# A gated cross-attention block with its feed-forward: the mask as one row, row maxima in fp16, constants and squares moved, the down product one unit further behind

## What is computed

```
logits  = einsum(Q, K) + b[0] + -1e30 * (1 - mask)
weights = softmax(logits);  out = weights @ V
x = x + tanh(g_xattn) * attention(ctx, layernorm(x), mask)
gate = x' @ wg.T / 127 ; up = x' @ wu.T / 127      # x' = layernorm(x)
x = x + tanh(g_ffn) * (silu(gate) * up) @ wd.T / 127
```

## Time and profile before

| what | value |
|---|---|
| median of 3 runs | 160.29 us (159.06 to 160.47) |
| the profiled execution | 158.84 us, span 157.0 us |
| PE busy | 132.8 us (85%) in 1363 matmuls |
| VectorE (DVE) busy | 122.4 us (78%) in 348 |
| ScalarE (ACT) busy | 92.9 us (59%) in 203 |
| GpSimd (POOL) busy | 90.9 us (58%) in 139 |
| mean granted TensorE clock | 0.994 |

### The profile page before, as it was taken

How to read it: one execution, slowest core, us unless ns; L and a number is a source line. 1 busy time by engine, 2 the same in 40 slices (tenths; PEclk the granted TensorE clock), 3 DMA queues, 4 the chain that set the end, 5 groups by cost and what they waited for, 6 DMA issues and landing times.

```text
span 157.0 us, 4000 instructions
## 1 busy us (share of the span) xinstructions
PE 132.8 (85%) x1363; PEld 99.9 (64%) x1363; DVE 122.4 (78%) x348; ACT 92.9 (59%) x203; POOL 90.9 (58%) x139
## 2 busy tenths in 40 slices
PE   0656789957898997999899999998999998899970
PEld 0233557735477685858695878678777777676750
DVE  3799899999998988997899699567924937766631
ACT  4327789967556483738373748553877654465530
POOL 6254450542755794689465956645674678774530
PEclk9999999999999999999999999999999999999997
DMA  4499910000006002921171216250100020020022
GB/s 134 134 364 373 363 44 0 6 0 0 4 0 134 6 19 48 136 71 34 33 138 67 40 33 134 71 69 0 43 28 0 0 71 0 0 69 4 0 73 75
DMA packets 19928, 11.06 MB, mean 70 GB/s; under 512 B 13488, under 2 KB 19136, under 8 KB 19904
## 3 DMA queue, kind: packets, MB, share of 16 engines
q1 hardware_dynamic: 19728, 10.49, 25.6%
q10 hardware_dynamic: 176, 0.27, 0.5%
HBM read 5.51 MB, written 2.10 MB: 48 GB/s over the span
## 4 chain that ended last, share of the span: by engine, by line
PE 34%; DVE 27%; POOL 12%; DMA 11%; issue 10%; ACT 3%; SPq 1%; POOLq 0%; DVEq 0%; ACTq 0%
PE ps L1339 13%; DMA n_t<-norm 8%; PE ps L1361 6%; DVE neg_max L1019 4%; DVE stats L911 4%; DVE gated L1068 3%; DMA gates<-in_L_xattn_b_dram 3%; POOL norm L675 3%; POOL rstd L646 3%; POOL norm L668 2%; PE ps L1274 2%; PE ps L1268 2%; DVE x_sb L890 2%; PE ps L1288 2%; DVE h L1079 2%
## 5 line engine op out<-in xcount | busy, mean ns | idle before, releaser
L1339 PE MATMUL ps<-n_t,w_gu_t 128*128 128x256 f16 x384 | 49.9, 273 | 3.3 <-DMA n_t<-norm 2.2
L1339 PEld LDWEIGHTS ps<-n_t,w_gu_t 128*128 128x128 f16 x384 | 36.2, 98 | 13.1 <-DMA n_t<-norm 4.2
L692 POOL TENSOR_TENSOR h<-h 128x256 f16<-128x256 f32 x48 | 32.2, 673 | 15.0 <-ACT h L832 14.8
L823 ACT ACTIVATE tanh_h<-ps 128x256 f32<-128x256 f32 x48 | 18.3, 382 | 21.0 <-PE ps L1339 20.8
L1361 PE MATMUL ps<-w_d_t,h 128*128 128x256 f16 x192 | 28.3, 272 | 0.8 <-DVE x_sb L890 0.4
L1019 DVE TENSOR_REDUCE neg_max<-ps 128x4 f32<-128x512 f32 x32 | 21.5, 685 | 6.5 <-PE ps L1218 6.5
L1068 DVE SCALAR_TENSOR_TENSOR gated<-tanh_h,ps 128x256 f32<-128x256 f32 x48 | 19.7, 411 | 6.1 <-ACT tanh_h L823 6.1
L646 POOL TENSOR_TENSOR rstd<-var_eps,neg_half 128x2 f32<-128x2 f32 x16 | 11.1, 696 | 21.4 <-DVE var_eps L918 21.3
L776 ACT ACTIVATE probs<-ps,key_bias 128x512 f32<-128x512 f32 x32 | 21.9, 684 | 2.5 <-PE ps L1247 2.4
L832 ACT ACTIVATE h<-h 128x256 f16<-128x256 f32 x48 | 19.8, 412 | 5.7 <-DVE h L1079 5.2
L1079 DVE SCALAR_TENSOR_TENSOR h<-ps,gated 128x256 f32<-128x256 f32 x48 | 20.3, 424 | 1.7
(11 more groups left out here) (97 smaller groups left out, 203.8 us busy)
## 6 DMA issues: line engine op xcount, KB each, us to landing
x_sb<-in_x_dram SPq DMA_DIRECT2D x8, 256.0 KB, 8.8
out_dram<-x_sb SPq DMA_DIRECT2D x8, 256.0 KB, 2.1
kv<-in_ctx_dram SPq DMA_DIRECT2D x3, 256.0 KB, 8.3
w_raw<-in_L_ffn_w_gate_dram SPq DMA_DIRECT2D x1, 768.0 KB, 7.3
w_raw<-in_L_ffn_w_up_dram SPq DMA_DIRECT2D x1, 768.0 KB, 9.1
w_raw<-in_L_ffn_w_down_dram SPq DMA_DIRECT2D x1, 768.0 KB, 8.4
kv<-in_ctx_dram ACTq DMA_DIRECT2D x1, 256.0 KB, 3.5
q_stacks<-q_parts SPq DMA_TRANSPOSE x8, 3.2
```

Of the source, the lines that this page charges most:

```text
L692: pool.tensor_tensor(h16[:, r % 2, m, 1, :], h32[:, n % NHB, :], h16[:, r % 2, m, 0, :], ALU.subtract).then_inc(h_low, 1)
L823: act.activation(tanh_h[:, n % 2, :], bank32(HID_BANKS[n % 2])[:, 0:SH], ACT.Tanh, scale=0.5 * W_SCALE).then_inc(tanh_done, 1)
L1339: ins = pe.matmul(dst, lhs, rhs, start=(w == 0 and (k, l) == terms[0]), stop=(k, l) == terms[-1], skip_group_check=True)
```

## The change

- **Mask.** The last 128 mask values of each batch are loaded once more as one row on one partition (`mask_row`, issued on ACT's queue ahead of the old mask load) and turned by one DVE step (`bias_row`) into 0 or -42496 in bf16. The mask matmul of `row_max` now has this one row and one row of ones as operands (contraction of 1 instead of 128), still 512 columns. The exp takes `exp_bias` (per key, four columns), made by `mask_t` and `exp_bias`, two small steps later on. The three-part bf16 split (`mask_parts`), the transposes and ACT copy of `mask_rows` leave the narrow path.
- **Maxima.** The reduction writes the negated maximum straight as fp16 (`max_cols16`); `max_split` leaves the narrow path, and `max_t` transposes fp16 and waits for the last reduction. The selector is fp16 too. `K_LIMIT` falls to 7500 (a constant in one clamp and one scale).
- **Order of the opening.** `k_parts 0` moves ahead of `norm1 0` on DVE, its low part from POOL to DVE (`k_rest`); 30 warm-up matmuls in six places (8, 2, 4, 4, 9, 3) stand for the 8 in one place, the first group before any other PE work; the mask transpose moves behind `q_stack 0 1`.
- **Loads.** The load of the keys and values of batch 0 moves from ACT's queue to SP's, behind the first x load; the three gates' loads move behind x 1 and kv 1.
- **Squares.** The ten square sums, one a chore, move from stages 0 to 1 to stages 3 to 6 (every second chore), `check` and `flag_sum` behind them to stage 6. `y_scale` stays where it was.
- **LAG** is 4 instead of 3; for the last six units the distance is 5 as before.
- One more memset (`max_cols16`) at the start of DVE.

```diff
-WARM_UP = 8
-K_LIMIT = 60000.0
+WARM_UP = (8, 2, 4, 4, 9, 3)
+K_LIMIT = 7500.0
+SHUT_OUT = -42496.0
...
-    steps = [("stats", 1, 0), ("mask_t",), ("warm_up",), ("norm1", 0), ("high", 1, 0), ("low", 1, 0), ("k_parts", 0),
-             ("mask_parts",), ("mask_rows",), ("dup", 0), ("stats", 1, 1), ("q_stack", 0, 0), ("k_stack", 0),
-             ("norm1", 1), ("q_stack", 0, 1), ("high", 1, 1), ("low", 1, 1), *maxima(0)[:3], ("dup", 1),
-             *maxima(0)[3:], sq(0), ("q_stack", 0, 2), ("max_split", 0), ("max_t", 0), ("q_stack", 0, 3),
-             ("k_parts", 1), ("stats", 1, 2)]
-
-    chores = [[sq(1)], [("w_cast", 0)], [sq(2), sq(3)], [("k_stack", 1)], [("w_t", 0), sq(4)],
-              [("w_cast", 1), ("w_t", 1), sq(5)],
-              [sq(6), sq(9)], [("w_t", 2)], [sq(7), ("w_t", 3)], [sq(8), ("check",)], [("flag_sum",), ("y_scale",)], [("w_cast", 2)],
-              [("w_t", 4)], [("w_t", 5)], [], [("k_parts", 2)], [("k_stack", 2)]]
+    steps = [("bias_row",), ("stats", 1, 0), ("warm_up", 0), ("k_parts", 0), ("norm1", 0), ("k_rest", 0),
+             ("high", 1, 0), ("low", 1, 0), ("mask_cast",), ("dup", 0), ("warm_up", 1), ("k_stack", 0),
+             ("stats", 1, 1), ("warm_up", 2), ("q_stack", 0, 0), ("q_stack", 0, 1), ("mask_t",), ("norm1", 1),
+             ("high", 1, 1), ("low", 1, 1), ("warm_up", 3), *maxima(0)[:2], ("exp_bias",), maxima(0)[2], ("dup", 1),
+             *maxima(0)[3:], ("warm_up", 4), ("q_stack", 0, 2), ("max_t", 0), ("q_stack", 0, 3), ("k_parts", 1),
+             ("stats", 1, 2), ("warm_up", 5)]
+
+    chores = [[], [("w_cast", 0)], [], [("k_stack", 1)], [("w_t", 0)], [("w_cast", 1), ("w_t", 1)],
+              [], [("w_t", 2)], [("w_t", 3)], [], [("y_scale",)], [("w_cast", 2)],
+              [("w_t", 4)], [("w_t", 5)], [], [("k_parts", 2)], [("k_stack", 2)], []]
+    chores += [part for i in range(10) for part in ([], [sq(i)])] + [[("check",)], [("flag_sum",)]]
...
-    LAG = 3
+    LAG = 4
...
-        put(("max_split", r + 1), when=ahead)
...
-        unit(n + i, LAG if i < 9 else LAG + 2)
+        unit(n + i, LAG if i < 9 else LAG + 1)
...
             load_x(sp, 0)
+            load_kv(sp, 0)
+            load_x(sp, 1)
+            load_kv(sp, 1)
             for n, g in enumerate((g_xattn, g_ffn, attn_b)):
                 sp.dma_start(gates[:, n:n + 1], g.partition_broadcast(P)).then_inc(gates_loaded, 16)
-            load_x(sp, 1)
-            load_kv(sp, 1)
...
+            act.dma_start(mask_row[:, :, :], mask[:, LAST * P:SK].unsqueeze(0)).then_inc(mask_row_loaded, 16)
             act.dma_start(mask_raw[:, :], mask.rearrange("b (c k) -> (b c) k", k=P)).then_inc(mask_loaded, 16)
-            load_kv(act, 0)
...
+            def exp_bias_steps():
+
+                dve.wait_ge(gates_loaded, 48)
+                mine(dve.tensor_scalar(exp_bias[:, :], exp_bias[:, :], MASK_STEP, gates[:, 2:3], ALU.mult, ALU.add))
+                wait_mine()
+
+                dve.tensor_scalar(exp_bias[:, :], exp_bias[:, :], gates[:, 2:3], 0.0, ALU.subtract, ALU.min
+                                  ).then_inc(exp_bias_ready, 1)
...
+                    elif kind == "bias_row":
+
+                        dve.wait_ge(mask_row_loaded, 16)
+                        dve.tensor_scalar(bias_row[:, :, :], mask_row[:, :, :], -SHUT_OUT, SHUT_OUT, ALU.mult, ALU.add
+                                          ).then_inc(bias_row_ready, 1)
...
+                    elif kind == "k_rest":
+
+                        b = step[1]
+                        dve.wait_ge(k_high, b + 1)
+                        full, high, low = key_parts(b)
+                        dve.tensor_tensor(low, full, high, ALU.subtract).then_inc(k_low, 1)
...
-                        rows = bias_rows[:, b * NC + c, :].unsqueeze(1).to_broadcast((P, HG, P))
-                        pe.matmul(bank32(n), ones_b[:, :], rows, start=False, stop=True, skip_group_check=True
+                        if is_wide:
+                            ones, rows = ones_b[:, :], bias_rows[:, b * NC + c, :].unsqueeze(1).to_broadcast((P, HG, P))
+                        else:
+                            pe.wait_ge(bias_row_ready, 1)
+                            ones, rows = ones_b[0:1, :], bias_row[:, b, :].unsqueeze(1).to_broadcast((1, HG, P))
+                        pe.matmul(bank32(n), ones, rows, start=False, stop=True, skip_group_check=True
```

More of the change, by code:

```diff
@@ L263, in narrow_steps @@
             put(("n_t", h))
-        unit(n + i, LAG if i < 9 else LAG + 2)
+        unit(n + i, LAG if i < 9 else LAG + 1)
         product(n + i)
     for n in range(len(units) + 1, len(units) + LAG + 2):
-        unit(n, LAG + 2)
+        unit(n, LAG + 1)
     return steps, split
@@ L274, in wide_steps @@
     R = 2 * B
-    steps = []
+    steps = [("mask_parts",)]
     for b in range(B):
@@ L379, in flamingo_block_kernel @@
         recip = sb("recip", [P, 2, NH], F32)
+        mask_row = sb("mask_row", [1, B, P], I32)
+        bias_row = sb("bias_row", [1, B, P], BF16)
+        exp_bias = sb("exp_bias", [P, B], F32)
+        max_cols16 = sb("max_cols16", [P, QT, P], F16)
+        max_rows16 = max_rows[:, :, :].rearrange("p n s -> p (n s)").bitcast(F16).rearrange("p (n s) -> p n s", n=2)
+        last_mask = mask_k[:, :].rearrange("p (b c) -> p b c", c=NC)[:, :, LAST]
+        max_sel16 = kv_rest[:, 0, :].bitcast(F16).rearrange("p (h k) -> p h k", h=NH)
         max_parts = max_cols[:, :, 0:NPART * NH].rearrange("p t (a h) -> p t a h", a=NPART)
@@ L675, in run @@
                         pool.tensor_tensor(low, full, high, ALU.subtract).then_inc(norm_low, 1)
-                    elif kind == "k_parts":
+                    elif kind == "k_parts" and step[1]:
                         b = step[1]
@@ L729, in run @@
                             act.activation(tanh_g[:, :], gates[:, 0:2], ACT.Tanh).then_inc(tanh_ready, 1)
+                    elif kind == "mask_parts":
+                        act.activation(max_sel[:, :, :], head_rows[:, :].unsqueeze(2).to_broadcast((P, NH, P)),
+                                       ACT.Copy).then_inc(selector_ready, 1)
                     elif kind == "mask_rows":
@@ L1011, in run @@
                         dve.wait_ge(work_filled, plan.filled(step))
-                        n = plan.nth[step[0].replace("row_max", "max_split"), 2 * b + qt // 2]
-                        if n >= 2 and qt % 2 == 0 and g == 0:
-                            dve.wait_ge(max_split, n - 1)
+                        h, first = 2 * b + qt // 2, qt % 2 == 0 and g == 0
                         if is_wide:
+                            n = plan.nth[WIDE + "max_split", h]
+                            if first and n >= 2:
+                                dve.wait_ge(max_split, n - 1)
                             dst = max_c[:, qt, g * HG:(g + 1) * HG, c]
                         else:
-                            dst = neg_max[:, qt, g * HG:(g + 1) * HG]
+                            if first and h == 0:
+                                dve.wait_ge(zeros_written, 1)
+                            if first and h >= 2:
+                                dve.wait_ge(work_filled, plan.filled(("max_t", h - 2)))
+                            dst = max_cols16[:, qt, g * HG:(g + 1) * HG]
                         dve.tensor_reduce(dst, bank32(plan.bank(step)).rearrange("p (h k) -> p h k", h=HG),
@@ L1021, in run @@
                     elif kind == "max_split":
-                        h, n = step[1], plan.nth[step]
+                        h = step[1]
                         b, qts = h // 2, slice(2 * (h % 2), 2 * (h % 2) + 2)
@@ L1127, in run @@
                     elif kind == "warm_up":
-                        for _ in range(WARM_UP):
-                            pe.matmul(bank32(SCORES[0]), ones_b[:, :], ones_b[:, :].unsqueeze(1).to_broadcast((P, HG, P)),
+                        for _ in range(WARM_UP[step[1]]):
+                            pe.matmul(bank32(Y_BANK), ones_b[:, :], ones_b[:, :].unsqueeze(1).to_broadcast((P, HG, P)),
                                       start=True, stop=True)
@@ L1246, in run @@
                                           stop=False, skip_group_check=True)
-                            ins = pe.matmul(dst, max_sel[:, h, :], max_rows[:, rows, :], start=False, stop=True,
+                            ins = pe.matmul(dst, (max_sel if is_wide else max_sel16)[:, h, :],
+                                            (max_rows if is_wide else max_rows16)[:, rows, :], start=False, stop=True,
                                             skip_group_check=True)
```

78 lines of the change are left out of this document (45 added, 33 removed).

## The result

The changed kernel takes **157.7 us** (median of 4 runs, 157.4 to 159.05) against 159.68 for the kernel before, run beside it: a ratio of 0.9887 [0.9845, 0.9928], a gain of some 2 us. The forecast was 155.4 us and a gain of 4.9. The direction is right, the size less than half, and 157.7 lies inside the stated range only because that range takes in the rivals. The profiled execution took 157.67 us, its span is 155.6 (before 158.84 and 157.0): between the two profiled executions the gain is only 1.2 us.

What follows compares the result with a forecast made beforehand. DVE bounds before 48 us, the ring from 60 to 106, then PE. Terms 0.75 + 3.3 + 1.0 - 0.2 - 0.2 - 0.1 = 4.55, taken as 4.9: median 160.29 to 155.4 us; own range 152.8 to 157.2, with rivals to 158.4.

Steps and rivals of the forecast that it cites:

- The rest: Remaining parts: mask matmul, fp16 transposes and selector 0 each; one moved down 0.2 lost, kv 0 load 0.1 lost.
- Opening, 0.75: Start of the kernel: mask split off DVE and reordering bring the second dup and first scores 0.75 us earlier.
- rival 3: Opening: the mask row lands late, at 5.0 us instead of 2.3, losing 2.5 us of gain: 157.9 us; chance 0.07.
- Stages 0 to 2, 3.3: 24 to 48 us: removing max_split, check and flag saves 3.8 us by DVE, 2.9 by PE; 3.3 taken.
- Stages 3 to 6, 1.0: LAG 4 moves finish behind stats, less a square ahead of tanh: net 0.3 a stage, 1.0 us in all.
- the ring: Stages 4 to 6: stats, rstd, norm2, low, DMA transpose, hidden, products, stats; period 15.45 us, forecast 15.1.
- Warm-ups, 0: Opening on PE: first groups cost 0.2, at most 1.2 us; the others fall in PE's waits; 0 taken.
- Rival 4: Opening: PE at 1.2 GHz, so about 1.0 us of its work takes twice that: 156.4 us; chance 0.05.
- (2): Squares ahead of tanh, 6.6 us if each is on the chain, make the kernel slower: 163.9 us; chance 0.05.
- (5): All DVE savings before 48 us are hidden by PE; result within 1% of 160.3 us; chance 0.05.
- Rival 1: 24 to 48 us: other DVE waits refill the hole; opening (0.75) and half the stages (1.7) remain: 158.0 us; chance 0.12.
- the smallest gain of 2.5: Lower end of the whole gain: PE's count, with squares and warm-ups each at their cost.

Runs made afterwards that it cites:

- squares back: The changed kernel with 128 mask rows, and the ten squares, check and flag_sum at their old places: 154.95 us, ratio 0.9699.
- the first-slot run: The changed kernel with 128 mask rows, and the squares three at a time in the first slot of stages 3 to 5: 154.44 us, ratio 0.9651.
- the last run: The changed kernel with 128 mask rows, squares in first slots, norm1 and exp_bias later, and check and flag_sum four slots later: 153.15 us, ratio 0.9594.

## Why the prediction was wrong in size

**The step that failed** is the first sentence of "The rest": "The mask matmul keeps its 512 columns ... 0 each". I priced the matmul by its columns and its own duration, and both did stay. What it costs its neighbours I didn't look for: 0.10 us before and behind it, up to 58 new changes of shape, 5.8 us of PE. Of these the end paid 2.9 us; that the rest fell where PE would have waited anyway is likely, but not followed wait by wait. By size this is the whole of the missing gain: the same change with 128 rows measures 154.77 us, and its ratio of 0.9703 makes 155.5 of the 160.29 that I started from, against a forecast of 155.4. That this agrees to 0.1 us is partly luck. The terms below miss in both directions, and the base was uneven: between the profiled executions, 158.84 and 154.88, the gain with 128 rows is 4.0 us, by the medians it is 5.3. The case was to be had beforehand, from the 0.31 behind the mask matmul where `weigh_o` follows. The rule that I weighed instead, the Trainium skill's that transposes don't count as PE work for the clock as matmuls do (TensorE: Matmul & The Clock Gate, Part 4: PE-mode transpose), decided nothing: the changed kernel's granted clock reads 1.00 from 24 us on in the stretches above, and no run here tells transposes from matmuls.

**Opening, 0.75.** The first scores start at 17.83 instead of 18.12: 0.3. From `norm1 0` (6.02, forecast 5.85) to `norm1 1` the steps came within 0.2 of the forecast. Then `exp_bias`, priced at 0.4 for two operations, took 1.0 and the DVE steps up to `dup` came late; with it moved away, the forecast holds to 0.1. The mask row came 0.5 us later than forecast: `bias_row` started at 3.53, not at 3.0, and `stats` at 3.87 instead of 3.72. That is far from the 2.5 us of rival 3, which is out.

**Stages 0 to 2, 3.3.** With the opening, 4.05 were forecast at the first product. The change as it is gave 1.96, with 128 rows 3.20, of which the squares and the flag are 1.43. The missing 0.85 with 128 rows is the 0.4 of `exp_bias` and some 0.4 of PE or DVE not told apart. PE has indeed no wait over 1 us between 30 and 36; the longest is 0.41. The first `hidden` behind the DMA, forecast at 56.5, starts at 58.44, and with 128 rows at 57.19.

**Stages 3 to 6, 1.0.** The places were wrong, and that the sum is nearly right with 128 rows, 1.08 from the first product to the end, is luck. LAG 4 gives 1.1 us of it, but at the end and not by taking `finish` out of the ring: the ring's `hidden` starts are 0.15 and 0.04 us later with LAG 4 than with LAG 3, not 0.65 a stage earlier. Two things stand beside this: the first `norm1` pair, which took 0.81 us with LAG 3, came to stand beside POOL's subtractions and took 1.95, and the DMA wait at 57.19 is still 1.28. The ring's turn was forecast at 15.1 us. It is 15.58 in the change as it is, 15.29 with 128 rows and 15.05 with the squares back as well (from one `hidden` to the next, one stage on). So the changes of shape account for some 0.3 of what is missing there and the squares for 0.2. The squares and the flag in stages 3 to 6 cost 1.04 where I took 0.3 a stage for the squares and 0.2 for the flag: about 0.3 for all the squares (the first-slot run), 0.8 for the flag (the last run), both by medians. The flag is the second mis-sized term, and its upper bound, 1.0, was the right end.

**What is left over.** With squares back and LAG 4 the part behind the first product is 2.12 us shorter than before. LAG explains 1.1. The other 1.0 may lie in `max_split` (which I took for hidden in the ring), in `finish`'s place or in the fp16 maxima; no run separates them, and the cause stays open.

**Warm-ups, 0.** In the profiled execution of the changed kernel that holds: the transposes behind the second `dup` start 0.64 us after it starts (before: 0.58). It doesn't always hold. With 32 and with 64 rows the first ten warm-ups take 4.45 us instead of 4.01, the groups behind them run on when PE could already do the work that follows, and those transposes start 1.23 us after the `dup`; hence the first scores at 18.69 and the 0.8 us of those two runs. With `exp_bias` moved it is 0.92. My bound of 1.2 us for the cost was right, the 0 was not. What I also missed is that they earn something: in this order PE's wait for the second `dup` is 2.75 us, and without the 22 late matmuls the clock fell in the traced execution and, by the mean clocks, in others. Rival 4 is in part what happened without them.

**Rivals 1, 2 and 5.** The gain up to the first product isn't lost to other waits of DVE (1); the squares aren't on the chain by 0.61 each (2); and the interval of the ratio excludes no effect (5). Rival 1's number, 158.0, was nearest to the result, for another reason. Two sums were off: by its own terms (0.75 + 1.7) rival 1 comes to 157.8, and so does the smallest gain of 2.5, where the forecast's own range ended at 157.2. The measured 157.7 lies at that end.

## What to carry to other kernels

Price a matmul by the distance to its neighbours' starts, not by its duration, and look at any edit that changes a contraction or an output width as one that adds two switches; padding with zeros up to the neighbours' 128 rows cost one memset here and won 1.9%. A small DVE step is priced by what POOL does beside it, and a serial flag by the product it stands in front of, not by its busy time. When an edit shows nothing in total, compare milestones: two effects of more than 1 us hid in the 0.2 us of the squares.
